# Attention maxima on one Trainium2 core: two key blocks per VectorE pass through a key difference

## What is computed

```python
energy = jnp.einsum('nqhd,nkhd->nhqk', Q, K) / jnp.sqrt(jnp.float32(HEAD_DIM))
attn = jax.nn.softmax(energy, axis=-1)
out = jnp.einsum('nhqk,nkhd->nqhd', attn, V).reshape(N, S, EMBED)
```

## Time and profile before

| | us |
|---|---|
| median of 3 runs | 1810.14 |
| lowest and highest | 1808.87 and 1810.49 |
| span of the profiled execution, first to last instruction | 1807.2 |

### The profile page before, as it was taken

How to read it: one execution, slowest core, us unless ns; L and a number is a source line. 1 busy time by engine, 2 the same in 40 slices (tenths; PEclk the granted TensorE clock), 3 DMA queues, 4 the chain that set the end, 5 groups by cost and what they waited for, 6 DMA issues and landing times.

```text
span 1807.2 us, 35352 instructions
## 1 busy us (share of the span) xinstructions
PE 1788.2 (99%) x13143; PEld 809.3 (45%) x13144; DVE 1489.3 (82%) x2716; ACT 1471.9 (81%) x1908; POOL 357.0 (20%) x441
## 2 busy tenths in 40 slices
PE   9999999999999999999999999999999999999997
PEld 5533333333333333333333333333326555699996
DVE  6889999999999999999999999999935422355553
ACT  6559999999999999999999999999997411254442
POOL 6655020020000000000000200001010177233333
PEclk9999999999999999999999999999999999999998
DMA  7534131232111121111313211133124733322221
GB/s 232 151 112 120 34 89 45 82 103 60 42 45 34 43 58 59 47 34 45 91 46 98 59 42 44 42 72 86 33 69 165 286 97 117 120 81 65 67 68 42
DMA packets 87294, 145.71 MB, mean 81 GB/s; under 512 B 18692, under 2 KB 53765, under 8 KB 87020
## 3 DMA queue, kind: packets, MB, share of 16 engines
q1 hardware_dynamic: 78220, 119.22, 22.2%
q0 software_dynamic: 7936, 23.10, 4.0%
q10 hardware_dynamic: 992, 1.44, 0.2%
HBM read 93.85 MB, written 50.36 MB: 80 GB/s over the span
## 4 chain that ended last, share of the span: by engine, by line
PE 84%; DVE 6%; DMA 5%; ACT 2%; POOL 1%; issue 1%; SPq 1%; POOLq 0%; DVEq 0%; ACTq 0%
PE ps L1218 25%; PE ps L1206 22%; PE ps L1149 14%; PE ps L1985 8%; DVE mx L1266 4%; PE ps L2008 4%; PE ps L727 3%; DMA sc_x<-n_rows 2%; DMA sorted_in<-sc_x,slot 2%; PE ps L1551 2%; PE ps L746 1%; ACT prob L1338 1%; PE ps L1521 1%; DVE mx L1277 1%; PE ps L1858 1%
## 5 line engine op out<-in xcount | busy, mean ns | idle before, releaser
L1266 DVE TENSOR_REDUCE mx<-ps 128x1 f32<-128x512 f32 x1588 | 1004.6, 684 | 11.6 <-PE ps L1149 7.4
L1338 ACT ACTIVATE prob<-ps 128x1024 f32<-128x1024 f32 x1024 | 992.8, 1021 | 3.3 <-issue 1.6
L1149 PE MATMUL ps<-k_high,q_high 64*128 64x512 bf16 x2048 | 577.5, 382 | 0.9 <-DVE mx L1266 0.2
L1218 PE MATMUL ps<-prob,vs 128*32 128x512 f32 x4096 | 545.5, 605 | 0.2 <-ACT head_out_sb L1344 0.2
L1206 PE MATMUL ps<-q_low,k_low 34*128 34x512 bf16 x2048 | 490.6, 377 | 0.0
L1206 PE MATMUL ps<-q_high,k_high 64*128 64x512 bf16 x2048 | 490.0, 376 | 0.5 <-ACT prob L1338 0.3
L1149 PEld LDWEIGHTS ps<-k_high,q_high 64*128 64x128 bf16 x2048 | 143.2, 93 | 547.1 <-DVE mx L1266 444.3
L1277 DVE TENSOR_REDUCE mx<-unit_sb 128x1 f32<-128x512 f32 x460 | 310.8, 676 | 0.0
L1317 ACT COPY unit_sb<-ps 128x512 f32<-128x512 f32 x460 | 269.6, 586 | 5.5 <-PE ps L1149 2.0
L1206 PEld LDWEIGHTS ps<-q_low,k_low 34*128 34x128 bf16 x2048 | 143.2, 94 | 118.7
L1367 POOL CAST mb<-turned_sb 16x128 bf16<-16x128 f32 x32 | 9.0, 283 | 826.4 <-ACT turned_sb L1324 814.9
(11 more groups left out here) (173 smaller groups left out, 1445.3 us busy)
## 6 DMA issues: line engine op xcount, KB each, us to landing
k_high<-qk_parts SPq DMA_DIRECT2D x126, 128.0 KB, 2.7
qk_parts<-parts SPq DMA_DIRECT2D x32, 384.0 KB, 3.0
k_low<-qk_parts SPq DMA_DIRECT2D x128, 64.0 KB
q_high<-qk_parts SPq DMA_DIRECT2D x126, 64.0 KB, 2.4
head_out<-head_out_sb SPq DMA_DIRECT2D x31, 256.0 KB, 2.2
sorted_in<-zero_row POOLq DMA_DIRECT2D x13, 390.0 KB, 4.6
xs<-sorted_in SPq DMA_DIRECT2D x39, 130.0 KB
q_low<-qk_parts SPq DMA_DIRECT2D x128, 32.0 KB
```

Source lines behind the costliest of these rows:

```text
L1149: pe.matmul(ps[:, ring.bank((n, m, u)), :], q_high[p][mine, t * P:(t + 1) * P], k_high[p][mine, c * CH:(c + 1) * CH], start=True, stop=Tru ...
L1218: mm = pe.matmul(ps[32 * j:32 * j + 32, 7, :], vs[buf(h)][:, kt, :], prob[:, (kt + 1) % 2, j * CH:(j + 1) * CH], start=(kt == 0), stop=(kt ...
L1266: dve.tensor_reduce(mx[n % 2][:, at, c:c + 1], ps[:, ring.bank(what), :], AX.X, ALU.max).then_inc(s_ring, 1)
L1338: act.activation(prob[:, (kt + 1) % 2, :].rearrange("p (u c n) -> p u c n", u=2, c=2)[:, :, half, :], ps[:, bank:bank + 2, :], ACT.Exp).th ...
```

## The change

The larger of two numbers x and y is y plus the positive part of x - y. The change uses this for key blocks 2 and 3 of unit 0, in each query tile: TensorE multiplies the queries with key block 2 **minus** key block 3 (a **step** product, in the place of block a), ScalarE writes its positive part to SBUF (`take_step`), and VectorE adds the block of keys 3 from PSUM to it and takes the maximum, in one pass (`tensor_tensor_reduce`). Two instructions come out of that pass, the pass and a read of its accumulated maximum. There are 8 such pairs of blocks in a head, in every other turn: a **step turn** has a step product for a and the fused pass for c, a **plain turn** has neither. In all, 245 step products and fused passes; the 460 copies of ScalarE and the 460 reductions of their copies go, and every block that was carried and isn't folded is reduced by VectorE from PSUM.

The key differences are made once for each batch: GpSimd subtracts and splits them into two bf16 parts (`key_steps`), they go to DRAM, and with each head's stacks two DMAs load its rows (`load_key_steps`). The weights `wuT` and `wdT` make room for this and are loaded in head 9, and the last expert's `rgT` is loaded behind the attention instead of in it. The order of the blocks, the ring of three banks and TensorE's number of matmuls stay.

```diff
-def carried(n, m, u):
-    return u == 0 and m % 2 == 1 and m != LEAD - 1 and (n >= 2 or n == 1 and m >= LEAD)
...
+def steps_of(n, m, u):
+    return u == 0 and m % CPB == STEP and (n >= 2 or n == 1 and m >= LEAD)
...
+def folded(n, m, u):
+    return u == 0 and m % CPB == STEP + 1 and steps_of(n, m - 1, u)
...
-                    self.add((n, m, u), "act" if carried(n, m, u) else "dve", count)
+                    self.add((n, m, u), "act" if steps_of(n, m, u) else "dve", count)
...
+        def key_steps(pool, step, half):
+            step(pool.tensor_tensor(k_from[half][:], k_from[half][:], k_to[half][:], ALU.subtract))
+            step(pool.tensor_copy(step_parts[half][:, 0, :], k_from[half][:]))
+            pool.tensor_tensor(step_parts[half][:, 1, :], k_from[half][:], step_parts[half][:, 0, :],
+                               ALU.subtract).then_inc(s_kstep, 1)
...
+                if n in STEPS_BEHIND:
+                    key_steps(pool, step, STEPS_BEHIND.index(n))
...
             for u in range(2):
                 stack_high(eng, h, u)
+            load_key_steps(eng, h)
             for u in range(2):
                 stack_low(eng, h, u)
...
+            keys = k_high[p][mine, c * CH:(c + 1) * CH]
+            if steps_of(n, m, u):
+                pe.wait_ge(s_kstep_in[n % 2], 32 * (n // 2 + n % 2))
+                keys = k_step[n % 2][mine, :]
...
+                if folded(*what):
+                    above = step_sb[steps_before(n, m - 1) % NSTEP][:]
+                    dve.wait_ge(s_turned, ring.taken((n, m - 1, u)))
+                    dve.tensor_tensor_reduce(above, bank, above, 1.0, LOWEST, ALU.add, ALU.max,
+                                             largest).then_inc(s_ring, 1)
+                else:
+                    dve.tensor_reduce(largest, bank, AX.X, ALU.max).then_inc(s_ring, 1)
...
+            act.activation(step_sb[k % NSTEP][:], ps[:, ring.bank(what), :], ACT.Relu).then_inc(s_turned, 1)
...
             def exps(n, kt):
                 act.wait_ge(s_prob_free, KT * n + kt + 1)
                 for half in range(2):
+                    if half and n + kt:
+                        take_step(act, n, kt)
...
-                    carry(act, KT * n + kt)
                     exps(n, kt)
...
-                if i < E and u == 0:
+                if i < E - 1 and u == 0:
                     pool.dma_start(rgT[:, bass.ds(i, 1)], io["rgT"][:, bass.ds(i, 1)]).then_inc(s_expert, 16)
...
+            sp.dma_start(rgT[:, E - 1:E], io["rgT"][:, E - 1:E]).then_inc(s_expert_late, 16)
```

More of the change, by code:

```diff
@@ L69 @@
 SLOTS = 6
-NCOPY = 2
+NSTEP = 2
+STEP = 2
+LOWEST = -3.0e38
 BESIDE = LEAD
@@ L397, in block_kernel @@
         s_turned = sem("s_turned")
-        s_carried = sem("s_carried")
+        s_kstep = sem("s_kstep")
+        s_kstepst = sem("s_kstepst")
+        s_kstep_in = [sem(f"s_kstep_in{i}") for i in range(2)]
         s_mb = sem("s_mb")
@@ L562, in unit, with kept, full @@
             return 2 * g + o // 2 if g < CPB and o % 2 == 0 else EARLY + 2 * g + o // 2 if g < CPB else UQ * g + o
+        def kept(g, o):
+            return o >= 2 and g % CPB in (STEP, STEP + 1)
+        def full(g, o):
+            return (k_from, k_to)[g % CPB - STEP][o - 2] if kept(g, o) else qf[unit(g, o) % UQ]
+        UNITS_AT = {unit(g, o): (g, o) for g in range(NCH) for o in range(UQ)}
         def adapt(pe, first):
@@ L695, in project_sync @@
                 sp.dma_start(dst[:], src).then_inc(s_late, 16)
+            for half in range(HALF):
+                store_key_steps(sp, 0, half)
             store(CPB + 1, 2, 3)
@@ L700, in project_sync @@
             store(CPB + 2, 2, 3)
+            load_key_steps(sp, (0, 1))
             maxima(sp, (0, 0))
@@ L1077, in prepare @@
                         sp.dma_start(xg_dram[c], xg[c][:]).then_inc(s_xgst, 16)
+                if n == XB_AT + 4:
+                    for half in range(HALF):
+                        store_key_steps(sp, 1, half)
+                if n == XB_AT + 5:
+                    sp.wait_ge(s_kstepst, 16 * HALF * B)
+                    for dst, name in ((wuT, "wuT"), (wdT, "wdT")):
+                        sp.dma_start(dst[:], io[name]).then_inc(s_shared, 16)
                 if n == XB_AT + 1:
@@ L1309, in carry @@
                 first, who = first - PAIRS, n + 2
-            if g < 2 or who >= NH:
+            if kt == 0:
+                first, who = LEAD + 2 * (KT - 1) - PAIRS, n + 1
+            what = (who, first, 0)
+            if who >= NH or not steps_of(*what):
                 return
-            what, k = (who, first + 1, 0), carried_before(who, first + 1)
-            if not carried(*what):
-                return
+            k = steps_before(who, first)
             act.wait_ge(s_max, ring.made(what))
-            wait(act, s_carried, k - NCOPY + 1)
-            act.copy(unit_sb[k % NCOPY][:], ps[:, ring.bank(what), :]).then_inc(s_turned, 1)
+            if k >= NSTEP:
+                act.wait_ge(s_ring, step_folded[k - NSTEP])
+            act.activation(step_sb[k % NSTEP][:], ps[:, ring.bank(what), :], ACT.Relu).then_inc(s_turned, 1)
+        step_folded = [ring.taken((n, m + 1, 0)) for n in range(NH) for m in range(PAIRS) if steps_of(n, m, 0)]
         def take_turned(act, n):
@@ L1427, in attend_gpsimd @@
                     bias(1, 0)
+                    for half in range(HALF):
+                        key_steps(pool, step, half)
                 if n == FIRST_AT + 6:
@@ L1488, in merge_sync @@
             store_x1(2)
-            sp.wait_ge(s_carried, carried_before(NH - 1, PAIRS))
+            sp.wait_ge(s_ring, ring.total["dve"])
             sp.dma_start(wgT[:], io["wgT"]).then_inc(s_shared, 16)
```

80 lines of the change are left out of this document (45 added, 35 removed).

## The result

| | us |
|---|---|
| before, median of 4 runs | 1810.27 (1808.87 to 1810.49) |
| after, median of 4 runs | 1899.64 (1899.60 to 1899.82) |
| after / before | 1.0494, 95% interval 1.0479 to 1.0509 |
| span of the profiled execution after | 1897.5 |

The change makes the kernel 4.9% slower, 89 us. The forecast was 1907 us, 97 above the median, with a range of 1872 to 1945. The span grew by 90.3 us.

What follows compares the result with a forecast made beforehand. TensorE's own stream, 2.41 us a turn, was taken as the bound. Thirty heads 93.0, head 30's turns 1.6 and edges 1 + 1 sum to 96.6 us: span 1903.8, median 2.9 above, 1907 us; range 1872 to 1945.

Steps and rivals of the forecast that it cites:

- TensorE's stream of 2.41 us is the bound: In attention turns, TensorE's own back-to-back stream takes 2.41 us a turn; VectorE and ScalarE are just under it.
- c taken by VectorE: In each of 16 turns, b waits 0.11 us for c's bank, where one turn a head has this wait before.
- The positive part hidden by 0.02: In a step turn it ends 1.77 us after a, freeing d's bank before d comes at 1.85; hidden by 0.02.
- The second exponential: In a step turn it ends at 2.70 us; the next scores start at 2.76, making b 0.23 to 0.24 late.
- The fused pass costs nothing: In step turns the accumulator's read adds 0.07 us (range 0 to 0.2), hidden under the second exponential's 0.23.
- The negation: Once a head, mneg ends 0.60 us later because c goes ahead of d; TensorE's transpose waits 0.49 us.
- The head: Each full head costs 2.61 us of turns plus 0.49 of negation, 3.10 us more; thirty heads make 93.0.
- The turns beside head 30: Maxima beside head 30 fill only turns 1 to 10: 5 x 0.34 - 0.11 = 1.6 us.
- The edges: GpSimd's six first key-step operations cost 1 us (0 to 3); the last expert's late weight load 1 us (0 to 2).
- The rivals: Among them, VectorE sets the attention's pace: 0.46 us saved 245 times, 113 us, giving 1697 us; 4% chance.
- TensorE keeps its own pace: Rival: b, scores and transpose in time, each head's 0.11 us goes, edges cost 2: 1809 us; 4% chance.
- only the ring waits: Rival: second exponential off the path, a head costs 15 x 0.11 + 0.49 = 2.14 us: 1877 us; 14% chance.

Runs made afterwards that it cites:

- the half passes: Kernel before, with VectorE's maxima and ScalarE's copies reading only 256 of each block's 512 columns: 1799.95 us, ratio 0.9963.
- the last set: Runs on one chip beside the kernel before (1806.18 us): VectorE's head copy with steps 0.998, without steps 1.0041, the changed kernel again 1.0492.
- the first experiment: Kernel before with ScalarE's copies gone and nothing in their place, VectorE reducing all 64 blocks of a head from PSUM: 1854.67 us, ratio 1.0268.
- the copy between the exponentials: Kernel before without ScalarE's copies, plus a useless SBUF-to-SBUF ScalarE copy between the exponentials of every other turn: 1901.49 us, ratio 1.0526.

## Why the prediction was right

The sign, the size and the mechanism held. That the sum came so close, 96.6 us for a span that grew by 90.3, is in part luck: the terms that were too large (the negation as it was added, the edges) are small, and the two errors in the ring's waits lay beside the chain that counts. By its steps:

- **TensorE's stream of 2.41 us is the bound.** Shown by the half passes (0.9963 with a third of VectorE's busy time gone) and by the kernel with the steps at c and the other c copied (0.9986). The wait of the weight load for VectorE, 444.3 us before, is 503.6 us after. In the kernel with half passes it is still 433.9 us, in turns of 2.41 us that wait for nothing, so most of it is no delay: the loader waits while the matmuls ahead of it still stream.
- **c taken by VectorE: 0.11 us forecast, 0.08 measured.** The 0.11 was read from one turn in which VectorE began the pass 0.08 after the product's end, since it was still at work on a carried copy. In the changed kernel it begins 0.03 after it (606.91 + 0.39 = 607.30, pass at 607.33). With the copies alone gone, 1.65 us a head were measured where 15 x 0.11 + 0.49 = 2.14 were forecast.
- **The positive part hidden by 0.02: wrong.** It ended when forecast (1.78 us after a, forecast 1.77), but the product that needs its bank started 0.14 after that, not 0.06, so c and d were 0.11 late. The forecast took the 0.06 from VectorE's release of a bank; the last section shows what lies between the two.
- **The second exponential: right to 0.02.** From a of a step turn, the first exponential starts at 0.27, the positive part at 1.19, the second exponential at 1.67 and ends at 2.70, and the scores start at 2.75 (forecast 2.70 and 2.76). b follows 0.45 later and the next a 1.97 after b: 5.17, in turns of 2.57 and 2.60 where 2.52 and 2.64 were named. This chain passes neither c's bank nor d's, which is why the two errors above did no harm. Forecast 5.15.
- **The fused pass costs nothing.** 692 ns, and the accumulator's read of 83 ns starts 0.61 behind the start of the pass and ends at the same time as it, within 0.01. The middle estimate of 0.07 extra was too high; both are hidden. The Trainium skill (Vector Engine (DVE) Microarchitecture Reference, Points that are easy to get wrong) halves the rate of such a pass for two fp32 sources in SBUF; with one of them in PSUM this trace shows the full rate.
- **The negation: 0.49 forecast, 0.49 measured, but added wrongly.** The forecast took 0.15 us from the negation's end to the transpose out of a gap in which TensorE was not waiting; that it measures 0.14 (621.67 to 621.81) is luck. The sum is where it goes wrong. While TensorE waits for the transpose, ScalarE gets ahead, so in turns 12 and 13 the waits on ScalarE vanish: 4.81 + 0.21 of the transpose itself + 0.49 + 2 x 0.08 = 5.67, as measured. The forecast would have had 5.15 + 0.21 + 0.49 = 5.85.
- **The head**: 41.83 - 38.83 = 3.00 us, forecast 3.10. Thirty heads make 90.0 in place of 93.0. Several heads of the kernel before are longer than 38.83 in its trace (the one that starts at 869.17 takes 39.83), after only two are longer than 41.83; that takes 2.5 us off. The turns beside head 30 cost 1.8, forecast 1.6. Together 89.4, as the windows show.
- **The edges**: forecast 1 + 1. The first exponential came 1.3 us earlier in this trace, at 129.24 in the repeated run of the same kernel against 129.37 before, so GpSimd's six operations cost nothing that can be seen. Behind the last exponential 2.2 us more were spent. On the chip of the last set, the same stretch of the changed kernel and of the kernel with VectorE's head copy and no steps, whose code there is that of before, take:

```profile
1455.66:1894.27 438.61, 425.64 (x2494) 339.51 (x2490) 193.43 (x489) 170.35 (x236) 162.57 (x206) 0.99 0.34 114
```

```profile
1372.14:1810.67 438.53, 425.54 (x2494) 339.52 (x2490) 192.88 (x489) 170.54 (x236) 162.90 (x206) 0.99 0.34 112
```

The difference is 0.1 us, so the late load of the last expert's weights costs next to nothing there, and the 2.2 us are not explained by it alone. No run shows the 1 + 1 of the forecast.
- **The rivals.** The Trainium skill (VectorE: DVE Perf Modes, Rules for kernel authors) lets chained VectorE work gain by fewer operations. VectorE has 8 passes fewer in a head here and 109 us less busy time, and the kernel is 4.9% slower; the rule doesn't bite where another engine's stream is the bound. "TensorE keeps its own pace" falls by the first experiment, in which the kernel without the copies, and without any step, is 2.7% slower, and "only the ring waits" by the copy between the exponentials.

## What to carry to other kernels

An engine that is 99% covered in a window is not yet the bound: look for a stretch in which its work is missing, and see whether the others run any faster there. Where a stream passes through a ring of few PSUM banks, look not at the work of the draining engines but at how long after its product each bank is freed; here, work taken off a second engine which drained in parallel cost time although it made both less busy. And of several waits in one cycle only the chain that closes last counts: follow it around in absolute times before adding delays up, since a wait that is taken away is often paid by the one behind it.

## What the runs showed that was not expected

- TensorE starts 0.14 to 0.15 us after ScalarE's end when it waits for the bank of a positive part (606.77 to 606.91, 717.53 to 717.68), but 0.05 to 0.06 after an exponential's (607.69 to 607.74) and after VectorE's reduction. The first product waits for two semaphores, and one of the waits stands on TensorE's queue as an instruction of its own, between 606.81 and 606.86, ahead of the weight load at 606.88:

```profile
L92 PEldq EVENT_SEMAPHORE  x1: 51/51/51, 606.8 to 606.8; - x1
```

The transpose, with two semaphores too, starts 0.14 after the negation when that wait ends last (621.67 to 621.81), and 0.06 after VectorE's pass in the kernel with the negation ahead, where the other does (619.27 to 619.32). So these four cases agree: the late one is the wait that has an instruction to itself.
- VectorE was all but a second bound of the kernel before: five reciprocals of 0.34 us more in a head made it 1.00 us longer, and one copy of 0.6 us more in each head made the kernel 0.4% slower.
- The read of the accumulator overlaps the pass that it reads: 83 ns, none of them on the path.
- A wait that the profile names can hide a second one of nearly the same length: the transpose's 0.49 us was 0.20 of negation and, under it, 0.29 of ring.
